# Projection block ends with four chunks sent and one stack asked for; the other sends follow the first maxima; moments come first in VectorE's turn

## What is computed

```
x = x + layernorm(attn(layernorm(x)));  x = x + layernorm(ffn(layernorm(x)))
attn:  c_q = x @ W_dq;   Q = c_q @ W_uq        # (4, 1024, 16, 8)
       c_kv = x @ W_dkv; K = c_kv @ W_uk; V = c_kv @ W_uv
       scores = Q K^T / sqrt(8), causal; softmax; @ V; @ W_o
```

## Time and profile before

| what | value |
|---|---|
| median of 3 runs | 1352.45 us (1351.22 to 1353.58) |
| the profiled execution | 1351.48 us, of which the span in the profile is 1349.7 us |
| busy over the span | PE 1225.1 us (91%), DVE 1112.1 (82%), ACT 922.2 (68%), POOL 760.5 (56%) |
| granted TensorE clock, mean | 0.967 of full speed |

### The profile page before, as it was taken

How to read it: one execution, slowest core, us unless ns; L and a number is a source line. 1 busy time by engine, 2 the same in 40 slices (tenths; PEclk the granted TensorE clock), 3 DMA queues, 4 the chain that set the end, 5 groups by cost and what they waited for, 6 DMA issues and landing times. The chain is left out here.

```text
span 1349.7 us, 30205 instructions
## 1 busy us (share of the span) xinstructions
PE 1225.1 (91%) x10501; PEld 705.7 (52%) x10501; DVE 1112.1 (82%) x2911; ACT 922.2 (68%) x2463; POOL 760.5 (56%) x770
## 2 busy tenths in 40 slices
PE   6389999999999999888899999799899999997895
PEld 3223434434443443356566666565466766665663
DVE  5488998998999898689899999766598999997675
ACT  6316776777777677578888888433588888885344
POOL 5212212332331233478999999532699999997244
PEclk9759999999999999999999999899999999998998
DMA  5430121112112101011111111100112111111001
GB/s 142 143 128 6 45 60 47 59 51 64 39 39 60 47 13 35 25 41 41 32 31 34 33 33 33 41 1 1 24 32 48 33 33 33 29 29 25 1 17 47
DMA packets 36286, 56.45 MB, mean 42 GB/s; under 512 B 6931, under 2 KB 23709, under 8 KB 33821
## 3 DMA queue, kind: packets, MB, share of 16 engines
q1 hardware_dynamic: 35440, 54.29, 15.0%
q10 hardware_dynamic: 696, 0.25, 0.1%
HBM read 27.78 MB, written 8.39 MB: 27 GB/s over the span
## 5 line engine op out<-in xcount | busy, mean ns | idle before, releaser
L1137 ACT ACTIVATE a_prob<-a_psE 128x512 f32<-128x512 f32 (+1 forms) x608 | 303.1, 591 | 134.5 <-PE a_psE L749 133.0
L1539 DVE CUSTOM_DVE_ANT_0 a_psM<-a_psM,mask_q 128x384 f32<-128x384 f32 (+3 forms) x512 | 234.6, 523 | 40.9 <-PE a_psM L733 40.3
L733 PE MATMUL a_psM<-a_ks,a_qs 72*128 72x512 bf16 (+3 forms) x768 | 241.3, 343 | 20.9 <-PEq L106 17.2
L1372 POOL TENSOR_SCALAR_AFFINE_SELECT a_prob<-a_prob 128x512 f32<-128x512 f32 x128 | 80.8, 638 | 309.3 <-ACT a_prob L1137 305.6
L749 PE MATMUL a_psE<-a_qs,a_ks 84*128 84x512 bf16 (+3 forms) x768 | 238.3, 333 | 12.1 <-ACT a_prob L1137 6.5
L1431 POOL TENSOR_TENSOR w_rn<-w_ssm,mhalf 128x16 f32<-128x16 f32 x64 | 220.5, 3445 | 50.8 <-DVE w_ssm L1631 35.5
L1247 ACT ACTIVATE w_prob<-w_psS,w_bias 128x128 f32<-128x128 f32 x512 | 180.3, 378 | 21.2 <-DVE w_bias L1657 21.1
L1416 POOL TENSOR_TENSOR w_t<-w_raw,w_sin 128x256 f32<-128x256 f32 x252 | 176.5, 732 | 0.0
L1541 DVE TENSOR_REDUCE a_nm<-a_psM 128x1 f32<-128x512 f32 x256 | 158.8, 682 | 14.9 <-PE a_psM L733 14.0
L1421 POOL TENSOR_TENSOR w_rot<-w_t,w_t 128x1024 f32<-128x1024 f32 x63 | 148.6, 2358 | 8.7 <-issue 0.4
L749 PEld LDWEIGHTS a_psE<-a_qs,a_ks 84*128 84x128 bf16 x768 | 74.5, 98 | 147.6 <-ACT a_prob L1137 76.2
(11 more groups left out here) (189 smaller groups left out, 2426.0 us busy)
## 6 DMA issues: line engine op xcount, KB each, us to landing
a_qs<-q_parts SPq DMA_DIRECT2D x16, 576.0 KB
a_ks<-k_parts SPq DMA_DIRECT2D x16, 576.0 KB
q_parts<-p_parts SPq DMA_DIRECT2D x24, 128.0 KB
k_parts<-p_parts SPq DMA_DIRECT2D x24, 128.0 KB
w_vb__719<-w_v__703 SPq DMA_DIRECT2D x16, 128.0 KB, 2.2
w_vb__720<-w_v__703 SPq DMA_DIRECT2D x16, 128.0 KB, 2.3
w_vb__720<-w_v__704 SPq DMA_DIRECT2D x16, 128.0 KB, 2.2
w_vb__721<-w_v__704 SPq DMA_DIRECT2D x16, 128.0 KB, 2.3
```

Source lines behind the costliest of these rows:

```text
L733: mm = pe.matmul(psM[:, m_bank(r), at:at + n], qs[0:ROWS, g, j, i * P:(i + 1) * P], ks[0:ROWS, g, j, 512 * kc:512 * kc + n], start=True, s ...
L1137: act.activation(prob[G % NPROB][:, j - share + 1:j + 1, 0:w], psE[:, r % NRING, 0:share * w].rearrange("p (j n) -> p j n", j=share), ACT. ...
L1539: d = dve.tensor_tensor_reduce(scores, scores, sb["mask_q"][:, 512 - n:512], -1.0, -3.0 * NEG, ALU.add, ALU.min, low)
```

## The change

Five things move, none is added to the arithmetic:

- SP's loads of x's later chunks go to ScalarE's queue, behind the weights; SP waits for chunk 3 of x before it loads the constants.
- In the projection block SP sends chunks 0 to 3 only, and asks for stack 0 behind them. Before, it sent six chunks, with stacks 0 and 1 among them.
- In the attention block SP asks for stack 1, waits for the first half of stage 0's maxima, and then sends chunks 4 and 5, asks for stack 2, sends 6 and 7, asks for stack 3.
- ScalarE sends the maxima of stage 1 too; SP did that.
- VectorE's turn has the moments ahead of remainder and low parts; POOL's has the powers ahead of the casts.

```diff
             sp.dma_start(sb["x"][:, 4:8, :], x_v[:, 4:8, :]).then_inc(x_in[1], 16)
-            sp.wait_ge(w_in, 16 * 6)
-            for c in (2, 3):
-                sp.dma_start(sb["x"][:, 4 * c:4 * c + 4, :], x_v[:, 4 * c:4 * c + 4, :]).then_inc(x_in[c], 16)
-            sp.dma_start(sb["x"][:, 16:NT, :], x_v[:, 16:NT, :]).then_inc(x_in[4], 16)
-
+            sp.wait_ge(x_in[3], 16)
...
-            for c in range(6):
+            for c in range(PARTS):
                 sp.wait_ge(parts_done, 2 * c + 2)
                 send_parts(sp, io, sb, c)
-                if c == 2:
-                    for first in range(2):
-                        sp.wait_ge(parts_out[first], 16 * 6)
-                    load_group(sp, io, sb, 0, 0)
-                if c == 4:
-                    load_group(sp, io, sb, 0, 1)
+            for c in range(2):
+                sp.wait_ge(parts_out[c], 16 * 6)
+            load_group(sp, io, sb, 0, 0)
...
                 act.dma_start(dst, src).then_inc(w_in, 16)
+            for c in (2, 3):
+                act.dma_start(sb["x"][:, 4 * c:4 * c + 4, :], x_v[:, 4 * c:4 * c + 4, :]).then_inc(x_in[c], 16)
+            act.dma_start(sb["x"][:, 16:NT, :], x_v[:, 16:NT, :]).then_inc(x_in[4], 16)
...
-            pipelined(pool, NCH, 2, [(3, middle), (0, powers)])
+            pipelined(pool, NCH, 2, [(0, powers), (3, middle)])
...
-            pipelined(dve, NCH, 2, [(1, shifts), (3, remainder), (3, low_q), (0, mean_and_weights), (3, low_k)])
+            pipelined(dve, NCH, 2, [(1, shifts), (0, mean_and_weights), (3, remainder), (3, low_q), (3, low_k)])
...
-            for c in range(6, NCH):
-                send_parts(sp, io, sb, c)
-            for g in range(2, NG):
+            for g in range(1, NG):
                 load_group(sp, io, sb, 0, g)
+                if g == 1:
+                    sp.wait_ge(nm_in[0], 16)
+                if g < NG - 1:
+                    for c in range(2 * g + 2, 2 * g + 4):
+                        send_parts(sp, io, sb, c)
...
             for e in range(NSTAGE):
-                if e + 1 < NSTAGE:
+                if 0 < e < NSTAGE - 1:
                     send_maxima(sp, e + 1, 0)
...
-                if e + 1 < NSTAGE:
+                if 0 < e < NSTAGE - 1:
                     send_maxima(sp, e + 1, 1)
...
                             copy_maxima(s, half)
-                            if s == 0:
+                            if s < 2:
                                 send_maxima(act, s, half)
```

## The result

The changed kernel took 1343.37 us (median of 4 runs, 1343.09 to 1346.66) against 1352.56 us for the kernel before beside it (4 runs, 1351.22 to 1353.58): a ratio of 0.9938, 95% interval 0.992 to 0.9956. That is faster by 9.2 us where the prediction had 16.1, and the median lies 0.37 us above its range. The profiled execution of after took 1343.09 us with a span of 1341.3, that of before 1351.48 with 1349.7. "Before" and "after" stand for the two kernels from here on, and a transfer has landed when the engine that waits for it can go on.

What follows compares the result with a forecast made beforehand. The prediction took the attention block's start, held by SP's sends blocked behind k stacks, as what can move. It summed 17.6 + 3.5 - 4 - 1 = 16.1 us off 1351.48, a median of 1336 us, range 1329 to 1343.

Steps and rivals of the forecast that it cites:

- The start: First score matmul of the attention block: at 49.6 us instead of 67.23, 17.6 us won.
- SP: SP's projection block ends at 38.1 us, no longer last; k stack asked for at about 37.9 lands at 48.3 to 49.1.
- The request: SP's asking for the first k stack, behind chunk 3's sends: forecast at about 37.9 us.
- the barrier: Engines' meeting point ahead of the attention block: forecast at 49.5 us, together with the k stack's landing.
- rival A: Attention start comes later, at 54: turn not shorter, chunk 3's send late, stack at 52 or more; 1340.8 us, chance 0.14.
- Rival B: Second half of maxima not delayed, TensorE at its higher clock sooner: 20 to 22 us won, 1330 to 1332; chance 0.12.
- The first half: First half of stage 0's maxima: lands at 62.6 us, VectorE's idle 3.53 goes; 3.5 us won (0 to 4.5).
- The second half: Second half of stage 0's maxima: sent at 81.4 us into a full queue, lands at 87.9; 4 us lost.
- The rule weighed in the prediction: Completion written only after the engine's earlier writes: second half waits for k stack 2, until 84 to 85 plus 2 us.
- ScalarE's sends: Two more sends of maxima on ScalarE, the first ahead of exponentials in a busy stretch: 1 us lost (0 to 2.5).
- C: Slower: second half lands only when SP's queue is empty, at 110.8 us; 1359 us, decided beyond 107.7; chance 0.03.
- D: Nothing won: another engine or transfer holds the barrier near 67 us; chance 0.02.

Runs made afterwards that it cites:

- e2: Changed kernel, with SP holding chunks 4 and 5 back until both halves of stage 0's maxima have landed: 1346.35 us, ratio 0.9947.
- e1: Changed kernel, with SP asking for stack 1 only once stack 0 has landed: 1341.0 us, ratio 0.9921.
- e4: Changed kernel, with VectorE's and POOL's turns of the projection block as they were before: 1346.49 us, ratio 0.9941.
- e5: Changed kernel, with stage 1's two sends of maxima back on SP: 1343.75 us, ratio 0.9943.
- e10: Changed kernel, with 8 extra matmuls on TensorE ahead of its wait for the second half of stage 0's maxima: 1343.24 us, ratio 0.992.
- e12: Changed kernel, with 16 extra matmuls on TensorE ahead of its wait for the second half of stage 0's maxima: 1342.43 us, ratio 0.9929.
- e6: Changed kernel, with each k stack asked for in three DMAs of 24 rows: 1338.78 us, ratio 0.9893.
- e9: Changed kernel, with SP asking for stacks 1 to 3 at once, then waiting for both halves, then sending chunks 4 to 7: 1343.69 us, ratio 0.9931.
- e11: Changed kernel: k stacks in three DMAs, stack 1 once stack 0 landed, stacks 2 and 3 between the halves, sends behind both: 1333.98 us, ratio 0.9863.
- e8: Changed kernel: k stacks in three DMAs, stacks 1 to 3 at once, then both halves awaited, then chunks 4 to 7: 1343.56 us, ratio 0.9932.

## Why the prediction came out as it did

The direction and the mechanism were right, and the sum for the profiled execution was 7.7 us too large (16.1 against 8.4 by the spans; by the medians it is 6.9): one term was mis-sized and one was missing.

**The start: 12.75, predicted 17.6. The step that failed** is in "SP": "The k stack is asked for at about 37.9 and, at 10.4 to 11.2 us, lands at 48.3 to 49.1". Those 10.4 and 11.2 us are the times after which the fourth send behind a stack released SP. In the kernel before no row showed the landing itself, and I took the release for it. e2 has both for one stack: release 10.4 us after asking, landing 13.3. From asking to the first matmul it is 13.9 alone (e1), 13.2 (e4), and 15.0 to 16.3 with stack 1 asked for behind it (after, e2, e5, e10, e12). The request itself was 1.4 later than forecast (39.30; chunk 3's sends run from 33.47 to 38.01 where 32.6 to 36.6 was forecast), but that did not decide: in e2 the stack was asked for at 37.75, as forecast, and the start is 54.01. Nor did the barrier, which fell 2.3 us earlier than forecast, at 47.2. With the landing made as short as the release (e6, 10.6) the start is the predicted one. The start fell near rival A's 54 with A's cause for the most part absent: the turn is 4.90, shorter than forecast, and ScalarE waited only 0.97 for chunk 3's send.

**The missing term: 2.8.** The sum carried times at either clock as if it would not change. The wait ahead of the second half puts the chain behind it on the low clock for some ten microseconds, where before had just left it. e12 and e2 show it from both sides: fill the wait or remove it, and the stretch takes 7.9 us instead of 10.7. Rival B had named the clock, as a gain; it was a cost.

**The first half: 3.5, right** (3.8 measured). The wait is gone.

**The second half: 4 lost, right** (4.1 measured, from sending it to VectorE's resumption). It is sent at 85.88, 4.5 later than forecast, for the late start, and lands 6.2 us later; the forecast had 6.5. Why it takes 6.2 is not settled. In the six kernels that have this order and one DMA for a k stack (after, e1, e4, e5, e10, e12) it lands 6.05 to 6.4 us after it was sent, 12.7 to 13.7 after stack 2 was asked for, and 2.3 to 2.95 after SP's blocked send is released. The rule weighed in the prediction (the Trainium skill, DMA: Bandwidth & Descriptors, "Queues, rings and completion order") says that a completion comes only after every earlier write of its engine, across queues. These traces agree with it so far as the half lands when a k stack would (13.2 to 13.9 after asking); e9 shows that this does not mean the end of every stack asked for before. The forecast's 84 for that end was too early on two counts: stack 2 was asked for at 78.97, not 74.0, and takes longer than 10.

**ScalarE's sends: 1 lost,** about right if the 0.5 us left at the high clock before the first copy are theirs, which no run shows; up to the second copy it is 0.5 more.

Together: 16.1 - 4.9 - 2.8 = 8.4, which is the difference of the spans; what else differs (0.3 more at the first half, 0.1 at the second, 0.3 lost behind the second copy) cancels. That it cancels so well is luck.

**C and D** did not happen: the second half lands at 92, far from 107.7, and nothing held the start near 67.

## What to carry to other kernels

When a queue's issue blocks and is released, don't take that for the landing of the transfer ahead: here the data came 2.9 us later. Look for a row in which an engine waits for the data, and if there is none, say that nothing bounds the landing from above. A small transfer on which an engine waits belongs into a moment in which no large one is in flight, even if another queue carries it; large ones fit between two such moments (e11). Price a wait on TensorE with what follows it at the lower clock, and ask of each shortened phase what it makes the next request run into.

## What the runs showed of the hardware

- A k stack as one DMA of 576 KB, at a fifth of the engines, is there 13.2 to 13.9 us after asking (e1, e4, e2's stack 2), while the send blocked behind such a stack is released after 10.3 to 11.2; in three DMAs of 24 rows it is there after 10.2 to 11.6 (e6, e8, e11), not three times sooner. With another stack asked for 8 to 9 us behind it, one DMA takes 15.0 to 16.3.
- 48 KB take 2.54 us in empty queues (before, e2, e8, e9, e11), and 6.05 to 6.4 with a k stack asked for 7 us earlier by another queue.
- TensorE's granted clock fell from 1.00 to 0.50 (2.4 to 1.2 GHz) after 1.53 us without work and stayed there for about 10 us (e10); after 0.17 us it did not fall (e12). After 0.86 us it fell once (e12, at 118) and did not once (after, at 121).
- A long issue on SP is not a measure of its own transfer: 7.98 us for a 128 KB send whose siblings take 0.5 to 2.3.
